# Second and third attention of a four-layer chain, from whole tiles to pairs of 64-row tiles

## What is computed

```
x = L0(x, ctx)    # 16 heads of 64; 256 x 256 scores; output projection, LayerNorm
x = L1(ctx, x)    # 16 heads of 16; 128 queries over 256 keys (ctx and latents), mask on the ctx keys;
                  # projection, RMSNorm, MLP 256-1024-256 with GELU, residual
x = L2(x, ctx)    # LayerNorm; 16 heads of 16; 128 queries over 128 keys, mask; projection;
                  # LayerNorm, MLP with GELU, residual
x = L3(x, ctx)    # 16 heads of 8; 256 x 256 scores; mean and std of the values under the
                  # attention; masked instance norm of x scaled by std and moved by mean
```

## Time and profile before

| | us |
|---|---|
| three runs | 1224.66, 1227.74, 1230.02 |
| median | 1227.74 |
| the profiled execution | 1224.94 |
| its span | 1223.1 |
| TensorE busy | 1044.4 (85%) |
| VectorE busy | 629.3 (51%) |
| ScalarE busy | 511.3 (42%) |
| GpSimd busy | 231.0 (19%) |

### The profile page before, as it was taken

How to read it: one execution, slowest core, us unless ns; L and a number is a source line. 1 busy time by engine, 2 the same in 40 slices (tenths; PEclk the granted TensorE clock), 3 DMA queues, 4 the chain that set the end, 5 groups by cost and what they waited for, 6 DMA issues and landing times.

```text
span 1223.1 us, 20508 instructions
## 1 busy us (share of the span) xinstructions
PE 1044.4 (85%) x7904; PEld 650.1 (53%) x7904; DVE 629.3 (51%) x1263; ACT 511.3 (42%) x993; POOL 231.0 (19%) x355
## 2 busy tenths in 40 slices
PE   7799889988899879997899888998789988987662
PEld 6466554665455654655546654466546556444430
DVE  1444644646536555456545474464654555555541
ACT  1423354344445344443543444443444434533233
POOL 0310012311213012131113102131111301222003
PEclk9899999999999999999999999999999998998787
DMA  9200020020100120002200102001110022000101
GB/s 376 91 1 30 40 93 25 8 74 24 70 31 1 73 83 25 16 2 74 92 17 16 72 3 92 29 3 74 52 50 23 1 73 84 16 16 5 69 1 35
DMA packets 26783, 59.96 MB, mean 49 GB/s; under 512 B 8120, under 2 KB 18752, under 8 KB 21824
## 3 DMA queue, kind: packets, MB, share of 16 engines
q1 hardware_dynamic: 26688, 58.65, 13.2%
HBM read 53.39 MB, written 5.24 MB: 48 GB/s over the span
## 4 chain that ended last, share of the span: by engine, by line
PE 49%; issue 30%; DVE 10%; POOL 8%; ACT 2%; DMA 1%; DVEq 0%; POOLq 0%; SPq 0%; ACTq 0%
DVE nm L1358 7%; PE PV L706 5%; PE SC L689 4%; PE GP L572 4%; PE GP L960 4%; PE GP L574 3%; PE GP L969 3%; PE GP L753 3%; PE GP L792 2%; PE SC L775 2%; PE GP L944 2%; PE MX L624 2%; PE MX L740 2%; PE PV L727 1%; PE MX L609 1%
## 5 line engine op out<-in xcount | busy, mean ns | idle before, releaser
L1358 DVE TENSOR_REDUCE nm<-MX 128x2 bf16<-128x512 f32 x256 | 165.2, 690 | 133.1 <-PE MX L630 81.1
L1157 ACT ACTIVATE Pr<-SC,bcol 128x512 f32<-128x512 f32 x128 | 81.2, 687 | 97.9 <-PE SC L775 97.9
L1685 POOL TENSOR_TENSOR Psum<-Pr 128x512 f32<-128x512 f32 x56 | 70.9, 1267 | 258.9 <-ACT Pr L1155 258.9
L572 PE MATMUL GP<-zP,W 128*128 128x128 f32 x512 | 106.1, 291 | 7.3 <-DMA W<-w 7.3
L1187 ACT ACTIVATE Pr<-SC,bcol 128x512 f32<-128x512 f32 x96 | 66.0, 688 | 102.1 <-PE SC L880 102.1
L1155 ACT ACTIVATE Pr<-SC 128x512 f32<-128x512 f32 x128 | 69.3, 594 | 91.3 <-PE SC L689 91.3
L880 PE MATMUL SC<-work,K 128*128 128x512 f32 x192 | 104.3, 625 | 0.0
L574 PE MATMUL GP<-uP,W 128*128 128x128 f32 x512 | 103.6, 286 | 0.0
L572 PEld LDWEIGHTS GP<-zP,W 128*128 128x128 f32 x512 | 84.1, 203 | 11.0 <-issue 9.3
L574 PEld LDWEIGHTS GP<-uP,W 128*128 128x128 f32 x512 | 82.3, 202 | 0.0
L1659 POOL TENSOR_TENSOR stat<-stat,half 128x1 f32<-128x1 f32 x24 | 13.6, 565 | 344.8 <-DVE stat L1493 270.9
(11 more groups left out here) (185 smaller groups left out, 1854.2 us busy)
## 6 DMA issues: line engine op xcount, KB each, us to landing
WA<-w1a SPq DMA_DIRECT2D x8, 1024.0 KB, 4.8
WB<-w1b SPq DMA_DIRECT2D x8, 1024.0 KB, 7.0
WA<-w2a SPq DMA_DIRECT2D x8, 1024.0 KB, 4.9
WB<-w2b SPq DMA_DIRECT2D x8, 1024.0 KB, 7.0
W<-w SPq DMA_DIRECT2D x6, 1024.0 KB, 10.2
scratch<-U SPq DMA_DIRECT2D x16, 256.0 KB, 2.0
C<-scratch SPq DMA_DIRECT2D x96, 32.0 KB
zP<-z_in SPq DMA_DIRECT2D x8, 128.0 KB, 2.1
```

The source lines that it names most:

```text
L572: pe.matmul(dst, W0[:, piece, 2 * s, at:at + P], zP[:, s * P:s * P + P], start=True, stop=False)
L1157: act.activation(Pr[:, (n + j) % 4, :], SC[j], ACT.Exp, bias=bcol[:, 3 + k % 2:4 + k % 2], scale=8.0 ** -0.5).then_inc(p_ready, 1)
L1358: dve.tensor_reduce(dst[:, g % 2, :, c:c + 1], MX[(n + i) % 2][:].rearrange("p (a k) -> p a k", a=2), AX_X, ALU.max, negate=True).then_inc ...
L1685: pool.tensor_tensor(Psum[:, c % 4, :].rearrange("p (a l) -> p a l", l=D), two[:, :, 0:D], two[:, :, D:2 * D], ALU.add)\
```

## The change

The second and third attentions now work on pairs of 64-row tiles too. Four heads lie in 64 rows, so four masked copies of the queries serve both halves, and Q12 has 8 blocks instead of 16. VectorE writes the bf16 blocks (Q12b) directly, GpSimd writes the fp32 blocks (Q12), both from qs; ScalarE casts nothing here, and the copy of the turned maxima goes from ScalarE to VectorE. A maxima unit fills both MX banks, a score step both SC banks. There are 4 score steps in the second attention and 2 in the third. VectorE's and GpSimd's parts of `end3`, ScalarE's `std3` and GpSimd's `output3` stand at other places.

```diff
-STEPS = {0: 4, 1: 2, 2: 1, 3: 4}
+STEPS = {0: 4, 1: 4, 2: 2, 3: 4}
...
-UNITS1 = [(1, g, u) for g in range(NG) for u in [*range(STEPS[1]), "T"]]
-UNITS2 = [(2, 0, 0), (2, 1, 0), (2, 0, "T"), (2, 2, 0), (2, 3, 0), (2, 2, "T")]
+UNITS1 = [(1, 0, 0), (1, 0, 2), (1, 0, "T"), (1, 1, 0), (1, 1, 2), (1, 1, "T")]
+UNITS2 = [(2, 0, 0), (2, 0, "T"), (2, 1, 0), (2, 1, "T")]
...
-                sp.dma_start(m1row[0:1, :], mask1[b]).then_inc(ld_msk, 16)
+                sp.dma_start(m1row[:], mask1[b].to_broadcast([P, P])).then_inc(ld_msk, 16)
...
+                def maxima_pair12(g, u):
+
                     n = MX_AT[b, L, g, u]
...
+                    for i in range(2):
+                        wait(pe, *mx_bank_taken(n + i))
+                    for i in range(2):
+                        half = slice(64 * i, 64 * i + 64)
+                        pe.matmul(MX[(n + i) % 2][:].rearrange("p (a k) -> p a k", k=keys), sel[half, 0, :],
+                                  mrow[half, :].unsqueeze(1).to_broadcast([64, per, keys]), start=True, stop=False,
                                   skip_group_check=True)
...
                     for j in range(per):
...
+                        for i in range(2):
+                            half = slice(64 * i, 64 * i + 64)
+                            mm = pe.matmul(MX[(n + i) % 2][:, j * keys:j * keys + keys],
+                                           Q12b[half, 4 * g + u // 2 * per + j, :], Kb[half, g, :],
+                                           start=False, stop=True, skip_group_check=True)
...
+            def attention12(b, L, make, K, V, v_ready, amid=lambda: None):
...
+                halves = 2 if L == 1 else 1
+
+                def scores(c, kc):
+                    n = SC_AT[b, L, 2 * (halves * c + kc)]
+                    if kc == 0:
+                        pe.wait_ge(*shifts(b, L, c))
+                        pe.wait_ge(s_Qx, 4 * b + 2 * (L - 1) + c + 1)
+                    for t in range(4):
+                        for r in range(2):
+                            half = slice(64 * r, 64 * r + 64)
+                            if t == 0:
+                                pe.wait_ge(p_ready, n - 1 + r)
+                            pe.matmul(SC[r][:, t * P:t * P + P], sel[half, 4 * c + t, :], nmT[half, c, :],
+                                      start=(t == 0), stop=False, skip_group_check=True)
+                    for r in range(2):
+                        half = slice(64 * r, 64 * r + 64)
+                        pe.matmul(SC[r][:].rearrange("p (t l) -> p t l", l=P), K[half, c, kc * P:kc * P + P],
+                                  Q12[half, 4 * c:4 * c + 4, :], start=False, stop=True,
+                                  skip_group_check=True).then_inc(sc_full, 1)
...
+                entry, then = (UNITS1[:4], [UNITS1[4:5], UNITS1[5:]]) if L == 1 else (UNITS2[:3], [UNITS2[3:]])
+                for _, g, u in entry:
+                    if (g, u) == (0, "T"):
                         amid()
                     make(g, u)
...
+                steps = [(c, kc) for c in range(2) for kc in range(halves)]
+                for i, (c, kc) in enumerate(steps):
+                    scores(c, kc)
+                    if i == 1:
                         pe.wait_ge(*v_ready)
+                    for _, g, u in (then[i] if i < len(then) else []):
+                        make(g, u)
+                    if i:
+                        pv(*steps[i - 1])
+                pv(*steps[-1])
...
+                for _, g, u in units:
                     if (g, u) == (0, "T"):
                         amid()
                     maxima(b, L, g, u)
...
+                after()
+                for g in range(NG):
+                    quotient(b, L, g)
...
-                for i in range(NG):
-                    dve.tensor_tensor(
-                        Q12[:, HG * i:HG * i + HG, :],
-                        qs[:, i // 2 * P:i // 2 * P + P].unsqueeze(1).to_broadcast([P, HG, P]),
-                        hmask[:, HG * (i % 2):HG * (i % 2) + HG].unsqueeze(2).to_broadcast([P, HG, P]), ALU.mult)\
-                        .then_inc(s_Qx, 1)
+                for c in range(2):
+                    dve.tensor_tensor(Q12b[:, 4 * c:4 * c + 4, :],
+                                      qs[:, c * P:c * P + P].unsqueeze(1).to_broadcast([P, 4, P]),
+                                      hmask[:, 0:4].unsqueeze(2).to_broadcast([P, 4, P]), ALU.mult)\
+                        .then_inc(s_Qxb, 1)
...
+            def blocks12(b, L):
...
+                pool.wait_ge(s_qs, 2 * b + L)
+                for c in range(2):
+                    pool.tensor_tensor(Q12[:, 4 * c:4 * c + 4, :],
+                                       qs[:, c * P:c * P + P].unsqueeze(1).to_broadcast([P, 4, P]),
+                                       hmask[:, 0:4].unsqueeze(2).to_broadcast([P, 4, P]), ALU.mult)\
+                        .then_inc(s_Qx, 1)
...
+                blocks12(b, 1)
                 pool.wait_ge(s_lat, b + 1)
                 pool.tensor_tensor(res1[:], lat, row("ob1"), ALU.add).then_inc(s_res1, 1)
                 pool.tensor_tensor(res2[:], lat, row("b2"), ALU.add).then_inc(s_res2, 1)
+                power(b, 1)
                 if not is_first(b):
                     norm3(b - 1)
                     end3(b - 1)
-                power(b, 1)
-                if not is_first(b):
-                    output3(b - 1)
 
                 power(b, 2)
                 pool.wait_ge(s_x1, b + 1)
                 pool.tensor_tensor(res1[:], x1[:], row("cb"), ALU.add).then_inc(s_res1, 1)
+                blocks12(b, 2)
+                if not is_first(b):
+                    output3(b - 1)
```

More of the change, by code:

```diff
@@ L1362, in maxima @@
[L1362 to L1372 removed]
+                n = MX_AT[b, L, g, u]
@@ L1571, in body @@
                 blocks12(b, o, 2)
-                attention(b, 2, lambda n: fill("qp2") if n == 1 else None)
-                for g in range(NG):
-                    quotient(b, 2, g)
+                attention12(b, 2, after=lambda: fill("qp2"))
                 g = take(o, "o2")
```

314 lines of the change are left out of this document (102 added, 212 removed).

## The result

The changed kernel takes 1243.52 us (median of 4 runs, 1242.03 to 1246.98), the kernel before 1226.38 us (median of 4 runs): ratio 1.014, 95% interval 1.0106 to 1.0174. The prediction, 1241.5 us and slower, is met.

A forecast was written before the change was run, and what follows sets the result against it. TensorE is 85% busy, but latency counts at the attentions' entries and ends. 8 x (-0.3) + 8 x 1.15 + 7 x 0.6 + 3 = +14 us on 1224.94, plus 2.8 to the median: 1241.5 us, range 1217 to 1261.

The forecast's parts named there:

- second attention: Second attention: the later entry is offset by pace and end; -0.3 us a batch over 8 batches, 0.1 us collision included.
- third attention, chain alone: Third attention: first products stand behind the second scores, so the first quotient starts at 712.4 instead of 711.26; +1.15 us a batch.
- first MLP, GpSimd's moved work: First MLP: norm3 and end3, now behind the root, delay VectorE's T products; +0.6 us in seven batches, ends -0.4 and +1.3.
- clock: Third attention and behind: one more half-speed TensorE stretch in every second batch, 0.8 us each; +3 us, ends 0 and 10.
- The signs that the prediction named: Trace marks of a right forecast: exponential pairs, first exponentials, query blocks, T products, TensorE busy down 50 us or more, longer span.
- The later entry: Second attention's start: maxima pairs fill both banks and delay qp0, so the first exponential comes 2.4 us later.
- the pace: Second attention: scores wait for both exponentials, so pairs of exponentials come 2.65 us apart (ends 2.5 and 2.9).
- the end: Second attention's end: two quotients in series where one stood; 679.2 against 679.57 before, -0.4 us a batch, -0.3 with the collision.
- The selectors: Second attention: seven of eight small selectors stand behind the second exponential, so the pace was taken as 2.65 us, not 2.5.
- The faster rival: Whole kernel: tiles overlap fully, no collision, exponential pairs 2.5 us apart; -1.5 us a batch, 1216 us. Chance 0.16.
- The query blocks: Attention starts: VectorE's and GpSimd's blocks exclude each other, 2.53 us; costs 0.1 us in the second attention, +1.15 instead of +0.35 in the third.
- the T products' collisions: First MLP: VectorE's two T products may each wait for one GpSimd instruction of 0.7 to 0.9 us.

The follow-up runs named there:

- kernel 5: Changed kernel with another order at the second attention's entry: latents and v1 column between the first two maxima pairs, qp0 later: 1220.63 us, ratio 0.9943.
- kernel 8: Kernel before plus ten fillers (matrix products no result uses) in the wait for the third LayerNorm alone: 1215.81 us, ratio 0.9901.
- kernel 10: Changed kernel, order as it is, plus 23 fillers in the third attention's pauses and ten in the third LayerNorm's wait: 1219.15 and 1218.97 us.
- kernel 1: Changed kernel, but GpSimd begins its two query blocks only when VectorE has finished its two: 1245.26 us, ratio to before 1.0147.
- kernel 2: Changed kernel, third attention's first product with the values ahead of the second scores: 1227.62 us, ratio 0.9976, runs in two groups.
- kernel 6: Changed kernel with both orders: third attention's values product ahead of second scores, and the second attention's new entry: 1208.79 us, ratio 0.9847.
- kernel 3: Changed kernel plus 23 fillers a batch (matrix products no result uses) in TensorE's pauses of the third attention: 1230.23 us, ratio 1.0022.
- kernel 9: Changed kernel plus ten fillers in the wait for the third LayerNorm alone: 1232.93 us, ratio 1.004.
- kernel 4: Changed kernel with GpSimd's norm3 and end3 put back ahead of the root power(b, 1): 1244.42 us, ratio 1.014.

## Why the prediction was right, and where it was not

| term of the sum | predicted, us | measured, us |
|---|---|---|
| second attention | -2.4 | -4.6 |
| third attention, chain alone | +9.2 | +5.7 |
| first MLP, GpSimd's moved work | +4.2 | -2.9 |
| clock | +3 (0 to 10) | +11.7 in the third attention, +7.1 behind it |
| sum | +14 | +17 |

The measured 5.7 is 8 x 0.71, from the 15.95 us of kernel 5, and 11.7 is what is left of 17.4: 13.9 us lost to the clock after the change, less the 2.2 that the last batch lost before. The 7.1 lies behind the third attention. Its 5.6 in the wait and from there to x are gone with fillers on both sides (kernels 8 and 10) and so are clock; the other 1.5, from x to the next `qs`, stay open.

The signs that the prediction named came in part. The pairs of exponentials, the later entry of the second attention, some T products above 0.69 us and a longer span with less TensorE work are as named, though TensorE's busy time fell by 47.9 us and not by 50. The slower query block took 1.53 us and not 1.9, and the first exponential of the third attention was not unchanged: it comes 6.33 us behind `qs` in one batch and 7.5 to 7.9 in the others, where it was 6.89. The range, 1217 to 1261 us, would have held a kernel as fast as before too, and 1238.9 + 2.8 makes 1241.7, not 1241.5.

- **Second attention: right.** The later entry (2.4), the pace (2.61 for 2.65) and the end (-0.5 a batch for -0.3, and -1.4 in the last batch) came nearly as worked out. The change's gain in pace was spent on its entry, and kernel 5 shows that this was a matter of order: 1.6 us a batch come back.
- **The selectors.** I took the pace from the exponential pairs and kept the page's rule as a rival. The rule held: seven selectors of 128 columns on two tiles take 0.18 us, where four of 128 columns on the whole array took 0.22, so one costs half as much. The trace thus agrees with the Trainium skill's page TensorEngine Tiling (Array Packing), section Key Properties, by which tiles load weights and multiply in parallel. The pace is 2.61 all the same: 1.26 us of ScalarE and 1.35 us of waiting for selectors, scores and their end, one behind the other. The faster rival, which needed 2.5, died here.
- **The query blocks: the step failed.** "0.63 + 1.27 + 0.63 = 2.53 us, and nothing is left of what the halving should give" was nearly right as a duration (2.14) and wrong as a cost. I had followed VectorE from its blocks to the maxima without asking what TensorE was doing: it had other products to finish until 1.8 us behind `qs`, and the maxima could start at 2.49 at best. The collision ended at 2.52 and so cost 0.03 us instead of the 0.8 that I had put (kernel 1). That was close: had GpSimd gone first, VectorE would have been free some 3.9 us behind `qs` (an estimate: 0.46 + 2 x (1.04 + 0.69)), 1.4 later than the maxima now start. VectorE's first block is undisturbed at 0.69 us and its second takes 1.53; the first one of GpSimd begins beside it. The Trainium skill's page SBUF — State Buffer, section Who interferes with whom, says that an instruction with two SBUF inputs contends with a GpSimd instruction that reads SBUF, and that the second to issue blocks; the durations of both engines' blocks (1.53 for 0.69, 1.51 for 1.04) agree, though 2.14 us is 0.28 less than strict turns would make (0.69 + 1.04 + 0.69).
- **The third attention's chain: right in kind, smaller.** The products behind the second scores put the first quotient later, as worked out: its gate comes 3.11 us behind the first exponential (kernel 5) against 1.83 before. But at full clock the first exponential comes 6.34 us behind `qs` instead of 6.89; 0.35 of that is the earlier start of the maxima (2.52 for 2.87). That makes +0.71 instead of +1.15. Kernels 2 and 6 confirm the cause by removing it: the gate comes 1.33 to 1.56 us behind the exponential.
- **GpSimd's moved work: wrong sign.** I priced the T products' collisions (0.6 us a batch). They occur, 1.20 us at most, but the stretch in which they lie (from the end of `xb` to x) grew by 0.1 us only. The larger effect I had only as one end of my range: the norm's product (`xb`) behind the root, 0.35 us now.

```profile
689.24 0.55 POOL L1594 TENSOR_TENSOR stat<-stat,half 128x1 f32<-128x1 f32 x1 [18.76 <-DVE stat L1482]
...
689.83 0.35 DVE L1485 TENSOR_SCALAR xb<-xa,stat 128x256 f32<-128x256 f32 x1 [0.67 <-POOL stat L1594]
```

Before, the same product took 0.81 us beside GpSimd's `output3`, which is the 0.4 us a batch by which this stage is shorter:

```profile
682.15 0.72 POOL L1651 TENSOR_TENSOR C<-C,xm 128x256 f32<-128x256 f32 x1
682.21 0.81 DVE L1558 TENSOR_SCALAR xb<-xa,stat 128x256 f32<-128x256 f32 x1 [0.69 <-POOL stat L1659]
```

- **The clock: the term that was mis-sized.** I added a half-speed stretch in every second batch from one window behind the third attention, +3 us, at most 10. It is 17 to 19 in the profiled execution. What I overlooked: a slowed stretch lies on the path where everything is serial, so the scores' 1.13 us become 2.06 at once; it comes in seven of eight batches; and the wait for the LayerNorm (4.0 us for 3.6) and, in two batches, the layer behind it (0.80 for 0.89) are slowed with it. Kernels 3 and 10 show this cause by removing it. Which pauses bring the clock down was not isolated.

The errors were -2.2 (second attention), -3.5, -7.1 and +15.8, if all of the 7.1 is put down to the clock; they left 3. The right total was thus in good part luck: the loss stands in the third attention, as I had put it, but the cause that I gave for it makes 5.7 of its 17.4 us.

## What to carry to other kernels

Work taken off an engine that is idle part of the time may show nothing until the order of its instructions lets the next engine start sooner: here two edits of order turned a change of +1.4% into -1.5%, and with the clock held into -2.8% (-2.0% against the kernel before with its ten fillers). Before pricing a delay on one engine, look up when the engine that waits for it is free. And where a change makes TensorE's pauses more frequent, read the granted clock stage by stage in both kernels, and give both the same fillers before comparing them: the kernel before gained 1% (11 us) from ten useless products a batch.

## What the runs showed of the hardware

- One program's times can lie in groups, up to 15 us apart, sorted by the granted clock (kernel 2: 0.946 to 0.948 and 0.918 to 0.926; kernel 9: 0.950 and 0.931 to 0.943). The kernel before does it on a smaller scale: 1223 to 1226 us at 0.961 and 1229 to 1230 at 0.954 to 0.956. A median of few runs of such a kernel says little.
- An edit in one attention changed the clock in the next one: with the third attention untouched, kernel 5 has it at 15.95 us in six batches and kernel 4 in four, where the changed kernel has it in one and 17.3 to 18.8 in the others.
- A GpSimd 128x512 fp32 product with two SBUF inputs takes 1.04 us alone and 1.51 beside VectorE's; the "1.27" that I took from the earlier trace rows is neither, because L1685 there is the sum of the probabilities and no product.
